# Stationary operands of three product families set to 128 columns in a gated cross-attention and spiking feed-forward kernel

## What is computed

```
x = x + tanh(g_xattn) * attn(ctx, layernorm(x))
    # xn = LN(ctx)*gm+bm (750 rows), ln = LN(layernorm(x))*gl+bl (224 rows)
    # q = ln @ Wq ; k, v = split(concat(xn, ln) @ Wkv) ; q = q / scale, scale = 64 ** -0.5
    # out = softmax(q @ k.T) @ v per head ; return out @ Wout
x = x + tanh(g_ffn) * spikes(layernorm(x))
    # h = relu(z @ W_fc.T) ** 2 ; y = h @ W_proj.T
    # 5 steps: mem = 0.9*mem + y - (mem > 1) ; spk = mem > 1 ; mean of spk
```

## Time and profile before

| | us |
|---|---|
| median of 3 executions | 1096.56 |
| lowest, highest | 1096.43, 1097.73 |
| the profiled execution | 1099.81 |
| its span (first to last instruction) | 1098.0 |
| TensorE busy with matmuls | 1060.3 |
| TensorE loading stationary operands (beside matmuls) | 869.7 |
| VectorE, ScalarE, GpSimd busy | 745.1, 589.9, 294.8 |

### The profile page before, as it was taken

One profiled execution on the slowest core, in us unless ns is written; L12 is line 12 of the kernel. 1 busy time (PEld: TensorE's weight loads), 2 busy tenths in 40 slices (PEclk: granted clock), 3 DMA queues, 4 the chain that ended last, 5 costly groups with the idle time before them and its releaser, 6 DMA issues.

```text
span 1098.0 us, 19326 instructions
## 1 busy us (share of the span) xinstructions
PE 1060.3 (97%) x7105; PEld 869.7 (79%) x7105; DVE 745.1 (68%) x1164; ACT 589.9 (54%) x1125; POOL 294.8 (27%) x270
## 2 busy tenths in 40 slices
PE   4999999999999999999999999997999999999996
PEld 3888878877887877887887787775788888998885
DVE  5567877877867787686787786768432555585765
ACT  5547646555744754764655584464544433445535
POOL 3024435324444353333532444323000000000000
PEclk9999999999999999999999999998999999999998
DMA  7301000201201101010020200122530000201011
GB/s 200 117 1 45 31 24 12 71 0 33 73 0 33 69 4 33 24 48 8 25 73 0 72 0 0 34 70 72 164 96 1 20 1 20 97 1 39 20 58 39
DMA packets 31511, 47.43 MB, mean 43 GB/s; under 512 B 2416, under 2 KB 10624, under 8 KB 31472
## 3 DMA queue, kind: packets, MB, share of 16 engines
q1 hardware_dynamic: 31132, 46.39, 13.1%
q10 hardware_dynamic: 340, 0.52, 0.2%
HBM read 39.56 MB, written 7.34 MB: 43 GB/s over the span
## 4 chain that ended last, share of the span: by engine, by line
PE 94%; DVE 3%; DMA 1%; issue 1%; SPq 0%; ACT 0%; DVEq 0%; ACTq 0%
PE work L438 53%; PE score L769 13%; PE heads_out L558 9%; PE score L521 8%; PE score L453 2%; PE maxes L543 1%; PE heads_out L570 1%; PE maxes L533 1%; PE score L783 1%; PE heads_out L438 1%; DMA xin<-in_x 1%; PE score L438 1%; DVE on L1333 0%; DVE probs L1286 0%; DVE top L1263 0%
## 5 line engine op out<-in xcount | busy, mean ns | idle before, releaser
L1723 POOL TENSOR_TENSOR dsum<-dsum,probs 125x448 f32<-125x448 f32 x186 | 225.1, 1210 | 14.6
L438 PE MATMUL work<-wv,xT 128*125 128x512 f32 (+1 forms) x768 | 187.2, 397 | 0.0
L438 PE MATMUL work<-xT,wk 128*128 128x488 f32 (+1 forms) x768 | 185.5, 392 | 0.6 <-DVE xT L1361 0.6
L438 PEld LDWEIGHTS work<-wv,xT 128*125 128x125 f32 (+1 forms) x768 | 137.7, 183 | 36.6 <-issue 2.3
L438 PEld LDWEIGHTS work<-xT,wk 128*128 128x128 f32 x768 | 140.3, 188 | 31.5 <-issue 4.6
L438 PE MATMUL work<-zT,wf 128*128 128x512 f32 (+1 forms) x768 | 164.0, 364 | 1.0 <-issue 1.0
L908 ACT ACTIVATE probs<-score 125x448 f32<-125x448 f32 (+1 forms) x256 | 119.9, 550 | 70.1 <-PE score L521 69.6
L438 PEld LDWEIGHTS work<-zT,wf 128*128 128x128 f32 x768 | 131.6, 189 | 23.8 <-issue 1.4
L1720 POOL TENSOR_TENSOR dsum<-probs 125x448 f32<-125x448 f32 x31 | 36.5, 1178 | 423.5 <-ACT probs L914 423.5
L1286 DVE TENSOR_TENSOR probs<-probs,maxes 125x1792 f32<-125x1792 f32 x64 | 128.2, 2013 | 6.4 <-PE maxes L543 5.9
L769 PE MATMUL score<-hT,wp 128*128 128x512 f32 (+1 forms) x576 | 117.7, 354 | 0.0
(11 more groups left out here) (178 smaller groups left out, 1422.4 us busy)
## 6 DMA issues: line engine op xcount, KB each, us to landing
xin<-in_ctx SPq DMA_DIRECT2D x42, 250.0 KB
neuron<-in_L_ffn_W_fc SPq DMA_DIRECT2D x16, 256.0 KB, 4.3
neuron<-in_L_ffn_W_proj SPq DMA_DIRECT2D x16, 256.0 KB, 2.8
xres<-in_x SPq DMA_DIRECT2D x16, 224.0 KB, 2.6
x_scratch<-xres SPq DMA_DIRECT2D x16, 224.0 KB, 2.3
out<-fin SPq DMA_DIRECT2D x14, 256.0 KB, 2.0
xin<-in_x SPq DMA_DIRECT2D x14, 224.0 KB, 9.4
zt<-x_scratch SPq DMA_DIRECT2D x3, 1024.0 KB, 6.0
```

What stands on the lines that cost most here:

```text
L438: mm = pe.matmul(bank, lhs(i, k), rhs(j, k), start=(n == 0), stop=(n == len(passes) * chunks - 1))
L1723: pool.tensor_tensor(total[0:ROWS[t]], total[0:ROWS[t]], tile(t), ALU.add).then_inc(dchain if t < TILES - 1 else dsum_done, 1)
```

## The change

Three families of products get a stationary operand of always 128 columns: `values`, `scores` and `out_projection`. Where a tile has 125 or 112 tokens, the slice now runs on into the next tile's tokens; behind the last token lie 16 new columns of zeros, so `xT` and `kst` become 990 columns wide and `oT` 240 (16 more, also zeroed). The outputs' extra rows in PSUM are written and read by nobody. Six small VectorE instructions at the start of the program write the zeros, by multiplying a tile of ones with 0. The row pitch of the three tiles grows by 64 bytes, and unused space (`spare2`) shrinks by as much, so that what lies behind `oT` keeps its place. The number and the order of matmuls, of waits and of DMAs stay as they are.

```diff
@@ constants and tiles
+    WIDE = AT[TILES - 1] + P
-        xT = sb(a, "xT", [P, 2, DC, KEYS], F32R)
-        kst = sb(a, "kst", [P, 2, 2, KEYS], F32R)
+        xT = sb(a, "xT", [P, 2, DC, WIDE], F32R)
+        kst = sb(a, "kst", [P, 2, 2, WIDE], F32R)
-        sb(a, "spare2", [P, 4 * L - D])
+        sb(a, "spare2", [P, 4 * L - D - 20 * (WIDE - KEYS)])
-        oT = sb(a, "oT", [P, 2, PAIRS, L], F32R)
+        oT = sb(a, "oT", [P, 2, PAIRS, LT + P], F32R)
@@ out_bank
-            return score[:, i, :] if isinstance(b, int) else work[i]
+            return score[:, i, :] if isinstance(b, int) else work[i][:, :]
@@ values
-                product(value_bank(t)[0:ROWS[t], :], lambda i, k: xT[:, i, k, AT[t]:AT[t] + ROWS[t]],
+                product(value_bank(t)[:, :], lambda i, k: xT[:, i, k, AT[t]:AT[t] + P],
                         lambda i, k: wv[:, i, k, :], DC).then_inc(v_mm, 1)
@@ scores
-                                mm = pe.matmul(score[0:ROWS[t], 2 * (k % 2) + e, t % 2 * L:(t % 2 + 1) * L],
-                                               kst[rows, s, i, AT[t]:AT[t] + ROWS[t]], qst[rows, s, j, :],
+                                mm = pe.matmul(score[:, 2 * (k % 2) + e, t % 2 * L:(t % 2 + 1) * L],
+                                               kst[rows, s, i, AT[t]:AT[t] + P], qst[rows, s, j, :],
@@ out_projection
-                    product(out_bank(b, i)[0:LT, :], lambda m, p: oT[:, m, p, i * LT:(i + 1) * LT],
+                    product(out_bank(b, i), lambda m, p: oT[:, m, p, i * LT:i * LT + P],
                             lambda k, p: wo[:, k, p, :], PAIRS).then_inc(wo_mm, 1)
@@ ScalarE and VectorE writers of oT (heads_hi, heads_lo)
-                act.activation(oT[:, 0, p, :], on32[:, :], ACT.Identity,
+                act.activation(oT[:, 0, p, 0:L], on32[:, :], ACT.Identity,
-                dve.scalar_tensor_tensor(oT[:, 1, p, :], on32[:, :], shift[:, 2, p, 0:1],
-                                         oT[:, 0, p, :].bitcast(F32), ALU.add, ALU.subtract).then_inc(o_done, 1)
+                dve.scalar_tensor_tensor(oT[:, 1, p, 0:L], on32[:, :], shift[:, 2, p, 0:1],
+                                         oT[:, 0, p, 0:L].bitcast(F32), ALU.add, ALU.subtract).then_inc(o_done, 1)
@@ VectorE, start of the program
             dve.wait_ge(const_ready, 4)
+            blank = ones[:, :].rearrange("p (k o) -> p k o", o=WIDE - KEYS)
+            for i in range(2):
+                dve.tensor_scalar(xT[:, i, :, KEYS:WIDE], blank, 0.0, None, ALU.mult)
+                dve.tensor_scalar(kst[:, i, :, KEYS:WIDE], blank[:, 0:2, :], 0.0, None, ALU.mult)
+                dve.tensor_scalar(oT[:, i, :, L:LT + P], blank, 0.0, None, ALU.mult)
```

## The result

The changed kernel takes 1099.55 us (median of 20 executions, 1098.37 to 1100.11), the kernel before 1096.97 us (median of 20, 1094.94 to 1098.40). The ratio is 1.0021, with a 95% interval of 1.0015 to 1.0028: slower by 2.3 us, 1.6 to 3.1. The prediction said 1099.6 us and slower by 0.27%.

A forecast was written before the change was run, and what follows sets the result against it. TensorE's stream was taken to bound the kernel; scores 3.0 us and 0 for the other terms, added to 1096.56, gave 1099.6 us, 0.27% slower. Forecast's own range 1098.3 to 1101.4; range leaving out at most 2 in 10, 1095.2 to 1101.5.

The forecast's parts named there:

- What bounds the kernel: Batch loop: TensorE, busy 97% of the span, sets the time one for one in seven of eight batches.
- Scores: Score matmuls: stationary loads of 128 columns, not hidden by 224 moving columns, add 3.0 us (bounds 2.4 to 4.8).
- the mean slope of 0.51 ns a column: Score pairs: 6.7 ns between 125 and 112 columns, giving 2.4 us; 3.0 taken for a steeper slope above 112.
- Quick loads: Rival, scores: 64-row loads at exactly 128 columns go quicker, 3.9 us less, 1092.7 us; chance 0.08.
- the scores' loads don't count: Rival, scores: the 6.7 ns come from fewer output columns or from neighbours, nothing changes, 1096.6 us; chance 0.07.
- Value products and output projection: 960 matmuls with 512 moving columns: load width hidden, stream stays unsettled, 0 us.
- the state of the stream: Value products and output projection: settled 226.7 ns or unsettled 231 to 233; uneven starts keep it unsettled, 0 taken.
- The rival of settled streams: Value products and output projections: full width lets streams settle, 3.2 us gained in eight batches, 1096.4 us; chance 0.20.
- Key and query products, and the pitch: Key and query products: shapes stay, pitch of xT goes from 974 to 990; 0, with 1 us to either side.
- VectorE's instructions, waits, buffers, DMAs: Program start: six instructions of about 0.6 us hidden behind a 3.75 us DMA wait; no waits or DMAs added; 0.

The follow-up runs named there:

- scores_only: Against the kernel before, only the scores widened to 128 columns, kst 990 columns wide with zeroed padding: 1099.67 us, ratio 1.0023.
- probe2: Kernel before plus TensorE-only streams with reordered start columns, then value and key products in the kernel's pass order: value products 231.6 ns narrow, 231.7 wide at pitch 974.
- pitch_only: Against the kernel before, only the row pitch of xT goes from 974 to 990 columns, all widths unchanged: 1096.19 us, ratio 0.9992.
- probe: Kernel before plus 34 appended TensorE-only streams varying start columns, widths and pitches: pairs with 224 moving columns take 104.4, 109.2, 111.7 ns at 112, 125, 128 columns.

## Why the prediction was right

**What bounds the kernel.** Right. TensorE's stream sets the time: what each edit adds to the stream shows in the batch's period, one for one.

**Scores.** Right in size and, as far as it was tested, in mechanism. Predicted 3.0 us, in the profile 3.2 (99.4 to 102.6 us of busy time, 0.40 us a batch in `scores_only`), in whole executions 2.5 (1.5 to 3.5). Both halves came to 1.53 us as forecast. The reason given for going above the mean slope of 0.51 ns a column was right too: pairs of 112 columns are held by something other than the width, which takes over at about 117, and above it the slope is 0.6 to 0.8. "Quick loads" fell: pairs of 128 columns are slower than pairs of 125, 111.7 against 109.2 ns, and their loads are on record with 187 ns. Of "the scores' loads don't count", the neighbours fell with `probe`, where the slope is there without them; that the number of output rows costs and not the load is what no run separates.

**Value products and output projection.** The term of 0 for the width was right: 0.3 ns or less a matmul in `probe2`, 0.02 us a batch in the kernel. The reason for it was only half right. The load's width is hidden there, as was said. For the state of the stream I took the nearest row to be the product whose slice starts at column 112, and blamed starts that aren't multiples of 128. Starts do decide, but not by that rule: 125 and 64 are as quick as 0 in rows of 512. The rival of settled streams fell, since the kernel's slices lie in rows of 974 or 990 columns, where no such state was reached. It wasn't empty, though: in rows of 512, from column 0 or 64, full width is what brings a stream from 233 to 226.7 ns. That no stream settled at the kernel's addresses was, for the forecast, in part luck. The product with `wv`, which I had counted for the rival, had 230.8 ns (a little less than the value product behind it, not "no less"); its start at column 0 may be why, which no run tested.

**Key and query products, and the pitch.** The step that was off. I had no row and took 0 with 1 us to either side; the pitch gave back 2.1 us in the key products (2.9 in `pitch_only`) and took 0.7 to 1.0 us in the value products. By the period the net is 1.6 us in `pitch_only`, and 1.2 between `scores_only` and the changed kernel (90.18 and 90.03 us). It lies outside my 1 us. It is why the whole change costs 2.0 to 2.3 us and not 3.2, and why my 1099.6 met the 1099.55 more closely than its terms deserved: it was reckoned from a median of 1096.56, which 20 executions put at 1096.97.

**VectorE's instructions, waits, buffers, DMAs.** Right: hidden. They took 0.17 to 0.27 us each rather than the 0.06 to 0.11 of their neighbours, 0.8 us in all, with more than 2 us of cover left.

**The working around the sum.** Two of its figures don't follow from their terms. 2.4 to 4.8 us with 1 us to either side is 1098.0 to 1102.4 us and not 1098.3 to 1101.4. And settled streams bring the sum under 0.2% (2.2 us) from about 100 ns a batch on, 0.8 us in eight, not from 160. Neither moves the 1099.6.

## What to carry to other kernels

Widening a stationary operand is free only where enough moving columns stand beside it: in this kernel's tiles 512 covered 128 stationary ones, 224 covered no more than about 117, and with 256 going from 112 to 128 still cost 6.5 ns a pair. Before padding a tile for the sake of its width, ask what the padding does to the rows' addresses; here the pitch moved 1.6 us, and the width of the value products and projections 0.2 us or less. Where a loop repeats, read its period from two far-apart pieces of the chain: it resolves 0.02 us a turn where whole executions scatter by 1 to 3 us.

## What the runs showed of the hardware

- Matmuls of the two-part float32 type with 128 by 512 run at 226.7, 229, 231 to 233 ns, and at 240 with an unevenly placed moving row, at one and the same granted clock (the 2.4 GHz level), with every other engine idle. Which it is depends on where the slices start, on how wide they are and on the rows' pitch, and once a stream has settled it repeats to 0.2 ns. The Trainium skill, "TensorE: Matmul & The Clock Gate", section "Back-to-back issue gap", gives N / 2.4 + 2.5 ns at full clock as the isolated gap from one matmul to the next, some 216 ns for 512 columns, and some 131 ns for a sustained stream; no stream here came under 226.7, and the measurement decides.
- A stream of key products with 488 and 486 moving columns at pitch 974 (223.8 ns) was hardly quicker than a full one of 512 in its best place (226.7 ns): the 24 or 26 columns left out saved 2.9 ns. By the slope from 256 moving columns (119.8 ns a pair in `probe`) to 512 (226.7), 0.42 ns a column, they would save some 10, an estimate.
- Two loads of 64 rows run beside each other: a pair of 128 columns with 224 moving ones takes 111.7 ns, and a single matmul of 128 rows with as many columns takes 111.5 (5.35 us for 48). A pair of 125 takes 109.2 ns in all, though each of its loads is on record with 185 ns. A load's recorded duration is therefore at least some 76 ns longer than the time for which it holds up the next one; only its slope over the columns could be used as a price.
- What in the placement of rows makes a stream quick wasn't found: starts 0, 64 and 125 were, 16, 32, 48, 96 and 112 weren't (11.01 us for 48 matmuls from column 48, 11.20 from 96).
